# The first weights and conditioning squares of an AdaLN-FFN kernel, issued in another order and by other queues

## What is computed

```
w = weights[conditions]                          # 128 x 32 x 32
h0 = einsum('bct,bcd->bdt', x, w)                # conditioning
h = square(relu(h0 @ up_w))                      # 256 -> 1024
y = h @ down_w                                   # 1024 -> 256
y += (h0 @ expert_weight) * sum(top_k(h0 @ gate_w, 2))
out = x + layernorm(y) * gamma + beta            # over the last axis, 256
```

## Time and profile before

| what | value |
|---|---|
| median of 3 runs | 229.66 us (229.6 to 229.78) |
| the profiled execution's own time | 229.29 us |
| its span | 227.6 us |
| PE (TensorE) busy | 220.9 us, 97% of the span |
| DVE (VectorE) busy | 160.9 us, 71% |
| ACT (ScalarE) busy | 106.4 us, 47% |
| POOL (GpSimd) busy | 131.4 us, 58% |
| mean granted clock of TensorE | 0.998 |
| moved by DMA | 11.81 MB |

### The profile page before, as it was taken

The page is one execution under the profiler, slowest core; times in us unless marked ns, Lnnn a source line. Parts: engine busy times, 40 slices in busy tenths (PEclk is TensorE's granted clock), DMA queues, the critical chain, the costliest instruction groups (busy, mean ns, idle before and its releaser), DMA issues.

```text
span 227.6 us, 3998 instructions
## 1 busy us (share of the span) xinstructions
PE 220.9 (97%) x1260; PEld 191.4 (84%) x1260; DVE 160.9 (71%) x352; ACT 106.4 (47%) x187; POOL 131.4 (58%) x131
## 2 busy tenths in 40 slices
PE   7899999999999999999999999999999999999992
PEld 2798888888888889888889888888888888888892
DVE  6587965777667777667667766577766766777885
ACT  3379865444555345534545444544454444444000
POOL 3758795665545763656455764366555575557411
PEclk9999999999999999999999999999999999999999
DMA  3877123030603010000200002000020002000031
GB/s 98 231 213 230 50 59 103 10 98 7 187 10 98 9 66 30 0 0 3 92 0 0 3 0 95 3 0 0 0 95 1 0 0 68 28 0 0 10 108 69
DMA packets 17177, 11.81 MB, mean 52 GB/s; under 512 B 6660, under 2 KB 16900, under 8 KB 17156
## 3 DMA queue, kind: packets, MB, share of 16 engines
q1 hardware_dynamic: 15460, 10.43, 15.1%
q10 hardware_dynamic: 1280, 1.07, 1.4%
q0 software_dynamic: 416, 0.05, 0.2%
HBM read 7.35 MB, written 4.19 MB: 51 GB/s over the span
## 4 chain that ended last, share of the span: by engine, by line
PE 94%; DMA 1%; issue 1%; DVE 1%; ACTq 1%; POOLq 0%; POOL 0%; ACT 0%; DVEq 0%
PE up_ps L337 39%; PE down_ps L431 25%; PE down_ps L433 13%; PE hid_ps L303 5%; PE moe_ps L449 3%; PE moe_ps L448 3%; PE moe_ps L447 3%; DMA wd<-in_L_cond_weights_dram 1%; PE down_ps L303 1%; ACTq L513 1%; DMA cond_row<-in_itok_B_dram 1%; POOLq L46 0%; POOL rstd L697 0%; DVE result L615 0%; DVE stats L588 0%
## 5 line engine op out<-in xcount | busy, mean ns | idle before, releaser
L682 POOL TENSOR_TENSOR sq_lo<-square,sq_hi 128x512 fp32r<-128x512 f32 x64 | 84.4, 1322 | 77.0 <-DVE square L553 77.0
L431 PE MATMUL down_ps<-down_hl,sq_hi 128*128 128x512 f32 x248 | 88.8, 393 | 0.0
L553 DVE SCALAR_TENSOR_TENSOR square<-up_ps,relu 128x512 f32<-128x512 f32 x64 | 44.0, 687 | 37.3 <-ACT relu L491 28.2
L433 PE MATMUL down_ps<-down_hl,sq_lo 128*128 128x256 f32 x248 | 69.6, 280 | 0.0
L431 PEld LDWEIGHTS down_ps<-down_hl,sq_hi 128*128 128x128 f32 x248 | 46.5, 188 | 10.8 <-issue 0.3
L491 ACT ACTIVATE relu<-up_ps 128x512 f32<-128x512 f32 x64 | 38.2, 596 | 35.8 <-PE up_ps L337 35.7
L337 PE MATMUL up_ps<-hid_hi,up_hi 128*128 128x512 f32 (+1 forms) x136 | 52.8, 391 | 0.3 <-ACT hid_hi L476 0.3
L337 PE MATMUL up_ps<-hid_hi,up_lo 128*128 128x512 f32 (+1 forms) x136 | 51.1, 379 | 0.0
L433 PEld LDWEIGHTS down_ps<-down_hl,sq_lo 128*128 128x128 f32 x248 | 46.7, 188 | 2.4
L493 ACT ACTIVATE sq_hi<-relu 128x512 fp32r<-128x512 f32 x64 | 40.6, 634 | 2.0
L337 PE MATMUL up_ps<-hid_lo,up_hi 128*128 128x512 f32 (+1 forms) x136 | 40.6, 381 | 0.0
(11 more groups left out here) (62 smaller groups left out, 193.3 us busy)
## 6 DMA issues: line engine op xcount, KB each, us to landing
x_sb<-in_x_dram SPq DMA_DIRECT2D x7, 512.0 KB, 4.2
out_dram<-result SPq DMA_DIRECT2D x7, 512.0 KB, 3.0
wd<-in_L_cond_weights_dram SPq DMA_DIRECT2D x111, 4.0 KB, 1.5
x_sb<-in_L_ffn_down_w_dram SPq DMA_DIRECT2D x2, 512.0 KB, 4.7
x_sb<-in_x_dram ACTq DMA_DIRECT2D x2, 256.0 KB, 2.9
result<-in_L_ffn_up_w_dram ACTq DMA_DIRECT2D x2, 256.0 KB, 2.9
result<-in_L_ffn_up_w_dram SPq DMA_DIRECT2D x1, 512.0 KB, 4.7
out_dram<-result SPq DMA_DIRECT2D x4, 128.0 KB, 1.7
```

Of the source, the lines that this page charges most:

```text
L431: pe.matmul(dst[:, :], a_hi, down_hl[:, c, :, :].rearrange("p s t -> p (s t)"), start=(c == 0), stop=False)
L433: mm = pe.matmul(dst[:, T:2 * T], a_lo, down_hl[:, c, 0, :], start=False, stop=(c == CH - 1))
L553: dve.scalar_tensor_tensor(square[:, c % 2, :], up_ps[c % UPB][:, :], 0.0, relu[:, c % 2, :], ALU.max, ALU.mult).then_inc(square_done, 1)
L682: pool.tensor_tensor(sq_lo[:, j % 2, c, :], square[:, c % 2, :], sq_hi[:, j % 2, c, :].bitcast(f32), ALU.subtract).then_inc(sq_lo_done, 1)
```

## The change

Up is still loaded in three pieces (0 to 255, 256 to 511, 512 to 1023 columns), but its last half is split in two pieces of two chunks each. The second piece of up is issued by SP right behind the first indices; the other indices follow behind SP's first four squares. SP's first squares are 0, 1, 4, 5, ScalarE's 2, 3, 6, 7, so that each of the two has two of either group. ScalarE then issues x of groups 2 and 3 and squares 8 and 9, and only after them rounds up's first quarter. SP issues squares 12 to 15. GpSimd issues squares 10 and 11, after x of groups 0 and 1 has landed. TensorE conditions group 2 once its squares are there and waits for group 3's afterwards. Of block 1's squares SP issues six and GpSimd ten. VectorE splits chunks 4 and 5 of up ahead of its loop and chunks 6 and 7 inside it, behind the split of the expert weights and behind the second chunk's square.

```diff
--- before.py
+++ after.py
@@ -19,7 +19,8 @@
 UPB = 4
 HALF = CH // 2
-UP_SPLITS = [slice(0, 2), slice(2, 4), slice(4, CH)]
+UP_LOADS = [slice(0, 2), slice(2, 4), slice(4, CH)]
+UP_SPLITS = [slice(0, 2), slice(2, 4), slice(4, 6), slice(6, CH)]
 DOWN_LOADS = 2
 DOWN_PARTS = 4
 DOWN_CH = CH // DOWN_PARTS
@@ -30,7 +31,10 @@
 SPLIT_DOWN_AT = {4: (0,), 5: (1,), 6: (2,), 7: (3,)}
-BY_SP, BY_ACT, BY_POOL, BY_SP_LATER = (0, 2, 4, 6), (1, 3, 5, 7), (8, 9, 10, 11, 12), (13, 14, 15)
+BY_SP, BY_ACT, BY_POOL = (0, 1, 4, 5), (2, 3, 6, 7), (10, 11)
+BY_ACT_LATER, BY_SP_LATER = (8, 9), (12, 13, 14, 15)
+
+SECOND_BY_SP = 6
 def adaln_ffn(nc, x, cond, cond_w, gate_w, up_w, down_w, expert_w, gamma, beta, out):
@@ -107,13 +111,13 @@
         x_first_landed = [sem(f"x_first_landed_half{h}") for h in range(2)]
         x_landed = {j: sem(f"x_landed{j}") for j in range(1, BLOCKS)}
-        up_landed = [sem(f"up_landed{n}") for n in range(len(UP_SPLITS))]
+        up_landed = [sem(f"up_landed{n}") for n in range(len(UP_LOADS))]
         down_landed = [sem(f"down_landed{n}") for n in range(DOWN_LOADS)]
         eg_landed, ln_landed = map(sem, ("eg_landed", "ln_landed"))
         cond_first_landed, cond_later_landed = map(sem, ("cond_first_landed", "cond_later_landed"))
-        wd_first_landed = [sem(f"wd_first_landed_group{g}") for g in range(TILES // 2)]
-        wd_later_landed = [sem("wd_later_landed_sp"), sem("wd_later_landed_pool")]
+        wd_first_landed = [sem(f"wd_first_landed_group{g}") for g in range(TILES)]
+        wd_pool_landed = sem("wd_first_landed_by_pool")
         wd_second_landed = [sem("wd_second_landed_sp"), sem("wd_second_landed_pool")]
         wd_landed = {j: sem(f"wd_landed_block{j}") for j in range(2, BLOCKS)}
@@ -219,9 +223,9 @@
         def weights_of(row):
             return cond_w[bass.ds(row, 1), :, :].rearrange("s c d -> (s c) d")
-        def load_up(queue, part):
-            cols = split_cols(part)
-            queue.dma_start(up_raw[:, :, cols], up_rows[:, :, cols]).then_inc(up_landed[part], 16)
+        def load_up(queue, load):
+            cols = slice(P * UP_LOADS[load].start, P * UP_LOADS[load].stop)
+            queue.dma_start(up_raw[:, :, cols], up_rows[:, :, cols]).then_inc(up_landed[load], 16)
         def load_x_first(queue, half):
             part = slice(TILES // 2 * half, TILES // 2 * (half + 1))
@@ -238,21 +242,22 @@
             cond_flat = cond.rearrange("(o b) -> o b", o=1)
             sp.dma_start(cond_row[:, 0:TILES * Q], cond_flat[:, 0:TILES * Q]).then_inc(cond_first_landed, 16)
-            sp.dma_start(cond_row[:, TILES * Q:ROWS_B], cond_flat[:, TILES * Q:ROWS_B]).then_inc(cond_later_landed, 16)
+            load_up(sp, 1)
             sp.wait_ge(cond_first_landed, 16)
             values = conditions(mybir.EngineType.SP, range(0, HALF_BLOCK))
             sp.wait_ge(wd_zeroed[0], 1)
             for b in BY_SP:
                 sp.dma_start(square_of(b), weights_of(values[b])).then_inc(wd_first_landed[b // Q], 16)
+            sp.dma_start(cond_row[:, TILES * Q:ROWS_B], cond_flat[:, TILES * Q:ROWS_B]).then_inc(cond_later_landed, 16)
             values = conditions(mybir.EngineType.SP, range(HALF_BLOCK, 2 * HALF_BLOCK))
             for b in BY_SP_LATER:
-                sp.dma_start(square_of(b), weights_of(values[b])).then_inc(wd_later_landed[0], 16)
+                sp.dma_start(square_of(b), weights_of(values[b])).then_inc(wd_first_landed[b // Q], 16)
             load_up(sp, 2)
             sp.dma_start(eg_raw[:, :, 0:T], expert_w.rearrange("(k p) h -> p k h", p=P)).then_inc(eg_landed, 16)
             sp.dma_start(eg_raw[:, :, T:EG], gate_w.rearrange("(k p) e -> p k e", p=P)).then_inc(eg_landed, 16)
             sp.dma_start(x_sb[:, groups(1), :], x_rows[:, groups(1), :]).then_inc(x_landed[1], 16)
             sp.wait_ge(cond_later_landed, 16)
-            second = range(TILES * Q, TILES * Q + HALF_BLOCK)
+            second = range(TILES * Q, TILES * Q + SECOND_BY_SP)
             values = conditions(mybir.EngineType.SP, second)
             sp.wait_ge(wd_zeroed[1], 1)
             for b, value in values.items():
@@ -313,18 +318,20 @@
                     condition(0, 0, 1).then_inc(hid_done, 1)
                     condition(0, 1, 1).then_inc(hid_done, 1)
                 else:
-                    pe.wait_ge(wd_later_landed[0], 16 * len(BY_SP_LATER))
-                    pe.wait_ge(wd_later_landed[1], 16 * len(BY_POOL))
-                    for k in range(K):
-                        condition(0, k, 2)
-                        condition(0, k, 3).then_inc(hid_done, 1)
+                    pe.wait_ge(wd_first_landed[2], 16 * len(BY_ACT_LATER))
+                    pe.wait_ge(wd_pool_landed, 16 * len(BY_POOL))
+                    condition(0, 0, 2)
+                    condition(0, 1, 2)
+                    pe.wait_ge(wd_first_landed[3], 16 * Q)
+                    condition(0, 0, 3).then_inc(hid_done, 1)
+                    condition(0, 1, 3).then_inc(hid_done, 1)
             def conditioning(j, k):
                 if k == 0:
                     pe.wait_ge(x_landed[j], 16)
                     if j == 1:
-                        pe.wait_ge(wd_second_landed[0], 16 * HALF_BLOCK)
-                        pe.wait_ge(wd_second_landed[1], 16 * HALF_BLOCK)
+                        pe.wait_ge(wd_second_landed[0], 16 * SECOND_BY_SP)
+                        pe.wait_ge(wd_second_landed[1], 16 * (TILES * Q - SECOND_BY_SP))
                     else:
                         pe.wait_ge(wd_landed[j], 16 * Q * TILES)
@@ -507,13 +514,14 @@
             load_x_first(act, 0)
             load_up(act, 0)
             act.wait_ge(cond_first_landed, 16)
-            values = conditions(mybir.EngineType.Activation, range(0, HALF_BLOCK))
+            values = conditions(mybir.EngineType.Activation, range(2, 2 + HALF_BLOCK))
             act.wait_ge(wd_zeroed[0], 1)
             for b in BY_ACT:
                 act.dma_start(square_of(b), weights_of(values[b])).then_inc(wd_first_landed[b // Q], 16)
+            load_x_first(act, 1)
+            for b in BY_ACT_LATER:
+                act.dma_start(square_of(b), weights_of(values[b])).then_inc(wd_first_landed[b // Q], 16)
             split_up(0)
-            load_up(act, 1)
-            load_x_first(act, 1)
             hidden_first(0, 0)
             hidden_first(0, 1)
             split_up(1)
@@ -620,6 +628,10 @@
                 dve.tensor_tensor(up_lo[:, :, split_cols(part)], up_raw[:, :, split_cols(part)],
                                   up_hi[:, :, split_cols(part)].bitcast(f32), ALU.subtract).then_inc(up_lo_ready, 1)
+
+            def round_up(part):
+                dve.tensor_copy(up_hi[:, :, split_cols(part)], up_raw[:, :, split_cols(part)]).then_inc(up_hi_ready, 1)
+
             def split_down(part):
                 dve.wait_ge(down_hi_ready, part + 1)
                 dve.tensor_tensor(down_hl[:, down_chunks(part), 1, :], down_raw[:, down_chunks(part), :],
@@ -639,7 +651,7 @@
             hidden_first(1, 0)
             hidden_first(1, 1)
             dve.wait_ge(up_landed[2], 16)
-            dve.tensor_copy(up_hi[:, :, split_cols(2)], up_raw[:, :, split_cols(2)]).then_inc(up_hi_ready, 1)
+            round_up(2)
             split_up(2)
             for j in range(BLOCKS + 1):
                 for c in range(CH):
@@ -651,6 +663,9 @@
                         dve.wait_ge(eg_hi_ready, 1)
                         dve.tensor_tensor(eg_lo[:, :, :], eg_raw[:, :, :], eg_hi[:, :, :].bitcast(f32), ALU.subtract) \
                             .then_inc(eg_lo_ready, 1)
+                        round_up(3)
+                    if j == 0 and c == 1:
+                        split_up(3)
                     if j == BLOCKS and c == 1:
                         moe_rest()
                     for block, t in tiles_at(j, c):
@@ -701,10 +716,12 @@
             pool.wait_ge(cond_first_landed, 16)
             values = conditions(mybir.EngineType.Pool, range(HALF_BLOCK, 2 * HALF_BLOCK))
             pool.wait_ge(wd_zeroed[0], 1)
+
+            pool.wait_ge(x_first_landed[0], 16)
             for b in BY_POOL:
-                pool.dma_start(square_of(b), weights_of(values[b])).then_inc(wd_later_landed[1], 16)
+                pool.dma_start(square_of(b), weights_of(values[b])).then_inc(wd_pool_landed, 16)
             pool.wait_ge(cond_later_landed, 16)
-            second = range(TILES * Q + HALF_BLOCK, 2 * TILES * Q)
+            second = range(TILES * Q + SECOND_BY_SP, 2 * TILES * Q)
             values = conditions(mybir.EngineType.Pool, second)
             pool.wait_ge(wd_zeroed[1], 1)
             for b, value in values.items():
```

## The result

The change makes the kernel slower: 232.85 us median (six runs, 231.8 to 234.39) against 229.63 for the kernel before beside it (229.15 to 229.95), a ratio of 1.0149, 95% interval 1.0112 to 1.0187. The forecast was 229.86, range 229.2 to 230.7. The time lies outside the range; the side of the late rival was right, its size was not.

The account below looks back on a forecast made before the run. TensorE was taken to bound the kernel (94% of the chain). Start 0 and chunk 4's wait -0.1 are lost in block 1's gate, +0.2, so 229.66 + 0.2 = 229.86, range 229.2 to 230.7.

Parts of the forecast that it names:

- the late rival: Block 1's gate: GpSimd's last squares land at 17.5, 0.9 behind the gate, giving 230.55; chance 0.24.
- Where: TensorE's head: start, wait before chunk 4 and block 1's conditioning count; the gate alone decides, +0.2.
- The step that failed: GpSimd, block 1: 1.25 from register load to first square, so first issue at 7.8, last of ten at 13.0.
- ScalarE: Head: four squares end at 4.99 as before, up's first-quarter split runs 6.5 to 7.16; start changes by 0.
- The latency: GpSimd's last square of block 1 takes 3.8 (bounds 1.9 to 4.5), landing at 16.8 instead of the gate's 16.6.
- Rival C: The late rival: GpSimd's last square takes 4.5 from 13.0, landing 17.5, 0.9 behind the gate; 230.55, chance 0.24.
- VectorE's idle time: Before chunk 4: square 0 starts at 13.5 instead of 13.65, gaining 0.1; the other piece runs after square 1.
- Up's second quarter: SP issues it at 1.34, hidden; group 1's last square still lands at 6.6, bounds 6.4 to 7.4.
- The median: Whole kernel: median 0.37 above the profiled execution; 229.5 forecast for the profiled one, 229.86 for the median.

Follow-up runs that it names:

- the traced run of six and ten squares: Kernel before, with SP issuing six and GpSimd ten of block 1's squares and GpSimd loading indices 16-32: 229.88 us, ratio 1.0016; the traced execution took 230.43.
- the version with GpSimd's squares out of the way: Changed kernel with both index loads aligned, ScalarE splitting up's first quarter before loading indices 8-16 and issuing squares 8 and 9: 230.39 us, ratio 1.0042.
- the nearest two: Changed kernel with both loads aligned and up's last half split in one piece, 229.93 us (1.0015); kernel before with six and ten squares, 229.88 us (1.0016).

## Why the prediction was wrong

- *Where.* Right in the main: the start and the gate at block 1 count, and in the changed kernel the gate swallows what comes before it. 2.56 at the gate is the whole loss of the profiled execution.
- *The step that failed:* "From the start of GpSimd's register load to its first square were 7.25 - 6.0 = 1.25". It was 9.30 - 6.36 = 2.94, since the load of ten indices from 22 takes 2.3 and that of eight from 24 takes 0.6. The sum took the load over unchanged, a term for the new range stood nowhere in it. The indices landed at 6.34 (6.6 taken), the ten squares are 0.575 apart as worked out, and the latency was 4.5 (3.8 taken): -0.2 + 1.7 + 0 + 0.7 = 2.2, and 16.8 + 2.2 = 19.0, the landing in the chain. The last issue, 14.48, lies outside its own bounds of 12.6 to 14.2. The same blindness in *ScalarE*, "Four squares end at 3.06 + 1.93 = 4.99, as before": they end at 6.1. I compared counts of instructions and never the ranges they read, though the diff shows both and the loads have a line in the trace.
- *The latency.* 3.8 was argued from a neighbour on another queue, with 4.5 on its own queue as the bound. Rival C's latency was there in the changed kernel (4.5) and in the traced run of six and ten squares (4.6), but the median of that run is only 0.2 above the kernel before. By itself this term explains 0.7 of the profiled loss, and rival C's price, 230.55, would have been too low as well. That the result lies on the side that C named is for the most part luck: its main cause is another, the load.
- *VectorE's idle time.* Where only the split was changed, square 0 came sooner (13.16), as worked out; in the changed kernel it came at 14.34, behind the late start. The second piece did not vanish in idle time: with the gate on time it costs 0.8 behind it. In the changed kernel the late gate hides that.
- *Up's second quarter.* Unchanged squares were wrong: 0.7 later alone, 0.15 in the version with GpSimd's squares out of the way.
- *The median.* The profiled execution missed its forecast, 229.5, by 2.3; the median missed its own by 3.0. The other 0.7 is that the median lies 1.05 above the profiled execution and not 0.37, by later landings and, in part of the executions, a lower clock behind a wait. Nothing in the sum stood for either.

No version tried beats the kernel before; the nearest two are slower by 0.15 and 0.16%. In the kernel before the start is held by the landing of the last squares (4.64 + 2.00), and the versions that took work off ScalarE's queue started no sooner than 7.89 against 7.74. Whether another order gains was not shown.

## What to carry to other kernels

When work is dealt out anew between queues, look at what each queue must load before its first issue, not only at how many issues it has: here two shifted index ranges cost 2.1 of 3.2 us, and reading from a multiple of four is faster even where it reads more than is used: 1.07 for 16-32 against 2.30 for 22-32, 1.2 for 0-16 against 1.95 for 2-10. An "idle" slot on one of two engines that exclude each other is only idle if the order of their starts stays as it is. The length of a wait of TensorE can be too low a price for it: in one of four traced executions its clock fell behind the wait and cost 1.6 us more.

## What was not expected of the hardware

- A register load from SBUF, with nothing beside it, takes 0.53 us for eight indices from 0 or 4 and 1.67 for eight from 1 or 2.
- GpSimd's difference and VectorE's expert split run one after the other but for 0.14 us: the same expert split takes 0.71 or 1.50 by who started first.
- A GpSimd square issued at 13.0 landed after 4.6, one at 13.46 in another version after 3.5.
- With 256 KB more on SP's queue, small transfers issued 3.3 us after it took 0.2 (ScalarE's) to 0.85 (SP's) longer, though the traffic fell to 21 GB/s just behind their issue.
